# The first stages of a fused gated-scan and butterfly-FFN kernel: coefficient parts stacked over lanes, loads and fold steps reordered

## What is computed

```python
def step(r, kv_t):                       # over time
    r = 0.9 * r + kv_t
    return (r, r)
kv = ctx * ctx
x = x + layernorm(x) * scan(step, kv)    # gate
h = layernorm(x) @ W_exp + b_exp
h = butterfly(h, up_weights, 2048)       # 11 stages of pairs i, i ^ 2**stage
h = gelu(h + up_bias)
h = butterfly(h, down_weights, 2048)
x = x + h @ W_con + b_con + down_bias
```

## Time and profile before

| what | value |
|---|---|
| median of 3 runs | 2817.45 us (2816.68 to 2817.59) |
| the profiled execution | 2817.23 us, of which span 2815.4 us |
| mean granted TensorE clock | 0.986 |
| TensorE busy | 2752.3 us, 98% |
| VectorE, ScalarE, GpSimd busy | 2135.5, 1144.9, 396.0 us |
| moved | 540.4 MB, mean 192 GB/s |

### The profile page before, as it was taken

One profiled execution on the slowest core, in us unless ns is written; L12 is line 12 of the kernel. 1 busy time (PEld: TensorE's weight loads), 2 busy tenths in 40 slices (PEclk: granted clock), 3 DMA queues, 4 the chain that ended last, 5 costly groups with the idle time before them and its releaser, 6 DMA issues.

```text
span 2815.4 us, 35216 instructions
## 1 busy us (share of the span) xinstructions
PE 2752.3 (98%) x12281; PEld 2276.5 (81%) x12281; DVE 2135.5 (76%) x3568; ACT 1144.9 (41%) x1690; POOL 396.0 (14%) x568
## 2 busy tenths in 40 slices
PE   7859999999999999999999999999999999999999
PEld 6738888888888888888888888888888888888887
DVE  7867778787877878787787878777787877788533
ACT  6643443434344343434334343433434343343432
POOL 4531102010110101011010101111010111102000
PEclk7879999999999999999999999999999999999999
DMA  8696484856757585665748566574856657585542
GB/s 207 166 319 189 156 239 152 226 176 191 209 169 228 152 239 164 200 206 169 222 153 249 163 198 200 176 211 154 250 165 201 204 168 215 151 248 164 182 150 98
DMA packets 293924, 540.44 MB, mean 192 GB/s; under 512 B 38718, under 2 KB 102366, under 8 KB 276854
## 3 DMA queue, kind: packets, MB, share of 16 engines
q1 hardware_dynamic: 287382, 534.80, 62.6%
q0 software_dynamic: 1520, 2.27, 0.4%
q10 hardware_dynamic: 4848, 1.13, 0.2%
HBM read 447.89 MB, written 56.62 MB: 179 GB/s over the span
## 4 chain that ended last, share of the span: by engine, by line
PE 94%; DVE 2%; SPq 1%; DMA 1%; ACT 1%; issue 0%; POOL 0%; DVEq 0%; ACTq 0%
PE ps L1482 43%; PE ps L1500 25%; PE ps L1513 25%; PE ps L1343 1%; DMA HX<-in_L_ffn_up_weights_dram 1%; ACT W1f L741 0%; SPq L450 0%; DVE w1r L998 0%; PE ps L1393 0%; PE ps L1382 0%; DMA w1r<-w_products 0%; SPq L429 0%; DMA w_products<-xop 0%; DVE raw L1100 0%; SPq L456 0%
## 5 line engine op out<-in xcount | busy, mean ns | idle before, releaser
L1482 PE MATMUL ps<-xop,w1r 128*128 128x512 f32 x5376 | 1365.1, 389 | 10.0 <-DMA w1r<-w_products 6.1
L1482 PEld LDWEIGHTS ps<-xop,w1r 128*128 128x128 f32 x5376 | 1009.9, 188 | 221.5 <-DMA w1r<-w_products 6.5
L1500 PE MATMUL ps<-w2r,ghi 128*128 128x512 f32 x2048 | 630.5, 389 | 0.0
L1513 PE MATMUL ps<-w2r,ghi 128*128 128x512 f32 x2032 | 626.4, 389 | 0.0
L854 ACT ACTIVATE st<-ps 128x512 f32<-128x512 f32 x384 | 229.8, 598 | 844.3 <-PE ps L1482 843.4
L1184 DVE TENSOR_TENSOR x<-ps,x 128x512 f32<-128x512 f32 x508 | 349.0, 687 | 281.7 <-PE ps L1513 279.1
L1500 PEld LDWEIGHTS ps<-w2r,ghi 128*128 128x128 f32 x2048 | 384.5, 188 | 79.7
L1513 PEld LDWEIGHTS ps<-w2r,ghi 128*128 128x128 f32 x2032 | 382.1, 188 | 79.3
L1202 DVE TENSOR_TENSOR g<-ps,st 128x512 f32<-128x512 f32 x384 | 263.1, 685 | 215.9 <-PE ps L1482 215.4
L858 ACT ACTIVATE g<-g,gelu_bias 128x512 f32<-128x512 f32 x384 | 275.4, 717 | 364.2 <-DVE g L1202 364.2
L1207 DVE TENSOR_TENSOR glo<-g,ghi 128x512 fp32r<-128x512 f32 x510 | 345.6, 698 | 78.3 <-ACT ghi L872 78.2
(11 more groups left out here) (140 smaller groups left out, 1659.5 us busy)
## 6 DMA issues: line engine op xcount, KB each, us to landing
w1r<-w_products SPq DMA_DIRECT2D x889, 256.0 KB, 3.2
w2r<-w_split SPq DMA_DIRECT2D x128, 1024.0 KB, 5.0
x<-in_x_dram SPq DMA_DIRECT2D x128, 256.0 KB, 7.1
raw<-kv SPq DMA_DIRECT2D x496, 64.0 KB, 2.1
out_dram<-x SPq DMA_DIRECT2D x120, 256.0 KB, 4.0
kv<-in_ctx_dram SPq DMA_DIRECT2D x64, 256.0 KB, 7.4
raw<-in_ctx_dram SPq DMA_DIRECT2D x64, 256.0 KB, 5.0
w_split<-w2s SPq DMA_DIRECT2D x12, 512.0 KB, 3.3
```

What stands on the lines that cost most here:

```text
L1482: last = nc.tensor.matmul(bank[:, :], w1r[:, slot, w, c * P:(c + 1) * P], xop[:, XPOS[m], v, c, :], start=(opens and i == 0), stop=(i == l ...
L1500: last = nc.tensor.matmul(ps_ya[j][:, :], g[:, p % 2, q, j * P:(j + 1) * P], w2r[:, p % 2, kk, w, :], start=(p == 0 and kk == 0 and i == 0 ...
L1513: last = nc.tensor.matmul(ps_yb[:, :], g[:, p % 2, q, j * P:(j + 1) * P], w2r[:, p % 2, kk, w, :], start=(kk == 0 and i == 0), stop=(kk == ...
```

## The change

- The parted coefficients: the high part goes to lanes 0 to 31 and the remainder to lanes 32 to 63 of one buffer, with the lanes of 0 to 31 zeroed first (VectorE for up, GpSimd for down, semaphore `parts_zeroed`) and the rounded `sel` copied to both lane groups. One matmul over 36 or 34 lanes replaces two; the buffer holds the pair's two halves one behind the other, so VectorE reads the spread result, and ScalarE and VectorE the source, with a stride. `csrc_c` is gone.
- The up set's coefficients and top move from SP's queue to the head of ScalarE's; the four W_exp quarters stand first on SP. The up set's high coefficients move from SP's to GpSimd's queue, ahead of the down set's. hc_up and the bias broadcasts are issued later by ScalarE.
- TensorE does up's high spread before low_up instead of behind it. ScalarE does coefs_hi(1) and the first square inside low_up, VectorE coefs_lo(1) and high_products(0) around the first scans.
- All high_dn and back copies go to ScalarE. GpSimd does rstd_rows(1) ahead of the first weight sums, and the bias additions only when eight low_dn steps are done.
- SP stores product sets 2 and 3 before the second moves. The second load of w2 and the first loads of context in the main part are issued behind reloads of w1.
- VectorE's token sums and remainders are put later among low_dn's steps.

The core of the diff, with "..." for what is left out:

```diff
@@ SP
-            load_wexp(0)
-            load_coefs(sp, up_w, 0)
-            load_top(sp, up_w, 0)
-            for q in range(1, 4):
+            for q in range(4):
                 load_wexp(q)
             load_tokens(kv, 0, ctx_rows, 0, ctx_loaded[0])
             load_tokens(xs[0], 0, x_rows, 0, x_loaded[0])
             load_top(sp, down_w, 1)
-            load_high(sp, up_w, 0)
...
             store_w1(0)
             store_w1(1)
+            store_w1(2)
+            store_w1(3)
             sp.wait_ge(xn_turned, 2 * J)
             move_xT(sp, 1, 0, xT_moved[1])
             move_xT(sp, 1, 1, xT_moved[1])
-            store_w1(2)
-            store_w1(3)
...
             load_w2(0)
-            load_w2(1)
...
-                    if go and p == 0:
-                        if first:
-                            sp.wait_ge(first_moved[1], FIRST_MOVES * NX)
+                    if go and p == 0 and not first:
                         sp.wait_ge(xT_moved[1], moved_by(u))
                         load_tokens(kv, 0, ctx_rows, u * 2 + 2, ctx_loaded[0])
                     for m in range(NM):
                         refill(u, p, m, last)
-                        if go and p == 0 and m == NM - 1:
+                        if first and p == 0 and m == 3:
+                            sp.wait_ge(first_moved[1], FIRST_MOVES * NX)
+                            sp.wait_ge(xT_moved[1], moved_by(u))
+                            load_tokens(kv, 0, ctx_rows, u * 2 + 2, ctx_loaded[0])
+                        if go and p == int(first) and m == (2 if first else NM - 1):
                             sp.wait_ge(xlo_ready, (u + 1) * NM)
                             load_tokens(raw[:, 1, :, :], 0, ctx_rows, u * 2 + 3, ctx_loaded[1])
...
-                    if not (first and p == 0) and not (last and p >= NP - 1):
+                    if first and p == 0:
+                        load_w2(1)
+                    elif not (last and p >= NP - 1):
@@ GpSimd
+            load_high(pool, up_w, 0)
             load_coefs(pool, down_w, 1)
+            pool.wait_ge(coef_spread, LOWS)
+            nc.gpsimd.memset(parts_zero(1), 0.0).then_inc(parts_zeroed, 1)
             load_high(pool, down_w, 1)
...
             first_moves(0)
+            rstd_rows(1)
             wait_kept(pool, "high_up", R - 1)
             weight_sums(0)
-            rstd_rows(1)
             weight_sums(1)
...
             pool.wait_ge(bias_row_ready, 1)
+            wait_kept(pool, "low_dn", KH // 2)
             add_bias(0, 0, xs[0])
@@ ScalarE
+            load_coefs(act, up_w, 0)
+            load_top(act, up_w, 0)
             act.dma_start(bias_rows[0:KH, :], ...)
             act.dma_start(bias_rows[KH:2 * KH, :], ...)
-            act.dma_start(hc_up, ...)
-            act.dma_start(bias_row[:, :], ...)
-            act.dma_start(bias_tmp, ...)
...
                 if k == KH // 4:
                     coefs_hi(0)
+                    act.dma_start(bias_row[:, :], ...)
+                    act.dma_start(bias_tmp, ...)
                     pick(0)
-                    coefs_hi(1)
                 fold_step("WT", k)
-            square(0, 0)
             for k in range(KH):
+                if k == 2:
+                    square(0, 0)
+                if k in (5, 8):
+                    coefs_hi(1, k // 8)
                 fold_step("low_up", k)
             pick(1)
             square(0, 1)
+            act.dma_start(hc_up, ...)
@@ VectorE
-            coefs_lo(1)
...
-            for j in range(J):
-                scan_chunk(0, 0, j)
+            scan_chunk(0, 0, 0)
+            scan_chunk(0, 0, 1)
+            coefs_lo(1)
+            scan_chunk(0, 0, 2)
+            scan_chunk(0, 0, 3)
+            high_products(0)
             stats1(0, 0, xs[0], range(J))
...
-            high_products(0)
             for j in range(J):
                 normalise(0, 0, xs[0], j)
...
-            fold_step("high_dn", 3)
...
-            fold_step("high_dn", 7)
...
-            for k in range(KH // 2):
-                fold_step("back", k)
             weights_lo(4)
-            for k in range(KH // 2, KH):
-                fold_step("back", k)
             tokens_lo(0, 0)
             tokens_lo(0, 1)
             weights_lo(5)
             token_sum(0, 0, first=True)
-            token_sum(0, 1, first=True)
             for k in range(4):
                 fold_step("low_dn", k)
             weights_lo(6)
+            token_sum(0, 1)
             for k in range(4, 8):
                 fold_step("low_dn", k)
             tokens_lo(0, 3)
-            token_sum(0, 2, first=True)
-            token_sum(0, 3, first=True)
             weights_lo(7)
             for k in range(8, KH):
                 fold_step("low_dn", k)
-            for m in (5, 2, 4, 6):
-                tokens_lo(0, m)
+            token_sum(0, 2)
+            tokens_lo(0, 5)
+            tokens_lo(0, 2)
+            token_sum(0, 3)
+            tokens_lo(0, 4)
+            tokens_lo(0, 6)
@@ TensorE
+                def parted_spread(place, stage):
+                    rows, off, n = src_place(stage)
+                    bank = place[0]
+                    for c in range(n // 1024):
+                        for bit in range(2):
+                            at = off + bit * (n // 2) + c * 512
+                            last = nc.tensor.matmul(ps[bank + c][:, :], sel_r[dn][0:Q + rows, stage - PARTED[0], bit, :],
+                                                    low_parts[dn][0:Q + rows, at:at + 512],
+                                                    start=(bit == 0), stop=(bit == 1))
+                    last.then_inc(coef_spread, 1)
...
+            spread_high()
             pe.wait_ge(low_matrix_ready, 1)
             for k in range(KH):
                 wait_kept(pe, "WT", k)
                 fold_step("low_up", k)
-            spread_high()
             spread_low_dn()
```

More of the change, by code:

```diff
@@ L299, in xattn_ffn_program, with low_part, low_whole, parts_zero @@
         PARTED = range(LOWS - 2, LOWS)
+        def low_part(dn, stage, lane):
+            rows, off, n = src_place(stage)
+            return low_parts[dn][lane:lane + rows, off:off + n].rearrange("q (b x) -> q b x", b=2)
+        def low_whole(dn, stage):
+            rows, off, n = src_place(stage)
+            return low_src[dn][0:rows, off:off + n].rearrange("q (x b) -> q b x", b=2)
+        def parts_zero(dn):
+            first, last = src_place(PARTED[0])[1], sum(src_place(PARTED[-1])[1:])
+            return low_parts[dn][0:Q, first:last].bitcast(f32)
         def spreads(dn, stage):
@@ L750, in coefs_hi @@
                     act.wait_ge(coef_spread, LOWS)
[L751 to L754 removed]
+                act.wait_ge(parts_zeroed, dn + 1)
+                for stage in PARTED if only is None else [PARTED[only]]:
+                    act.activation(low_part(dn, stage, 0), low_whole(dn, stage), ACT.Copy).then_inc(coef_hi, 1)
             def weights_hi(n):
@@ L947, in path_products @@
                         for c in range(banks):
-                            coef = ps[bank + c][:, col:col + m].rearrange("p (o a l) -> p o a l", o=outer // banks, a=2)
+                            order = "p (o l a) -> p o a l" if not first and stage in PARTED else "p (o a l) -> p o a l"
+                            coef = ps[bank + c][:, col:col + m].rearrange(order, o=outer // banks, a=2)
                             last = path_stage(nc.vector, cur[:, c * m:(c + 1) * m],
```

67 lines of the change are left out of this document (27 added, 40 removed).

## The result

The changed kernel takes **2823.62 us** (median of 12 runs, 2821.29 to 2827.72), the kernel before 2817.30 (12 runs, 2815.17 to 2818.63) on the same chip: a ratio of 1.0024, 95% interval 1.0015 to 1.0033. It is slower, by 0.24%. The forecast was 2805.4 with a range up to 2812.5: wrong in sign, and outside its range. The profiled execution took 2825.76 us, 2.1 over its median, with a span of 2824.0 us (before 2815.4).

A forecast was written before the change was run, and what follows sets the result against it. All behind 213.60 us, where TensorE's waits stop, was taken as constant. +6.4, -5.7 and -7.3 bring products 6.6 us earlier; with the end, that point becomes 201.8: 2817.2 - 11.8 = 2805.4 us, range 2797 to 2812.5.

The forecast's parts named there:

- wexp: Start: last wexp quarter, landing at 32.15 before, taken to land at 25 with hc_up and two bias broadcasts moved later.
- the path that the forecast said gives less: Before high_dn: later VectorE scans and statistics, then GpSimd's order holding ScalarE's first split to 111.1, against 113.0 by wcon.
- (a): Rival, start: wexp lands at 32, low_up starts 3 to 4 us later and all after it; 2809.4, chance 0.20.
- (b): Rival: front not late, as top lands as before or the clock holds, and token work overlaps; 2799.4, chance 0.17.
- (c): Rival, end: stores set it, last store stays near 194 and only 5.2 us count; 2812, chance 0.08.
- (d), the clock: Rival: TensorE at half clock in low_up, high_up and high_dn; 40 of 48 steps so would give 2836.4, chance 0.05.
- The middle: From first high_dn copy, ScalarE does all copies without wait: 38.7 us against 44.4, -5.7; then -7.3 to low_dn's last remainder.
- hc_up beside wcon: hc_up's packets issued beside the wcon load: between nothing and 5.4 us, taken as 2; wcon lands at 110.9.
- Stacking: In each spread 12 matmuls of 512 columns become 6, 2.7 us of TensorE covered by other waits: nothing gained.
- The end: Behind the first products: token instructions take 10.6 us against 4.63; first reloaded product at 197.7, no stall, 2.6 us half clock gone.
- My -7.3 for the late order: From split 5 to low_dn's last remainder, 34.2 us before: two token sums leave (4.3), the split falls from 5.3 to 2.3.

The follow-up runs named there:

- base: Changed kernel with up's six coefficient loads and top back on SP between the first and second wexp quarter: 2811.58 us, ratio 0.9979 to the kernel before.
- the runs on GpSimd's loads: Changed kernel with GpSimd waiting for up's coefficients to land before it issues its loads of up's high coefficients: 2823.03 us, ratio 1.0022 to the kernel before.

## Why the prediction was wrong, point by point

| point | forecast | changed kernel | base (coefs on SP) |
|---|---|---|---|
| low_up starts | 35.0 | 46.33 | 33.33 |
| wait for wcon ends | 110.9 | 120.49 | 107.65 |
| first products | 178.6 | 189.89 | 176.09 |
| third product after the first | 6.7 | 9.75 | 9.74 |
| first reloaded product | 197.7 | 211.98 | 198.82 |
| span | 2803.6 | 2824.0 | 2807.1 |

**The step that failed** is in the loads: "The top coefficients (2 MB) now share with wexp instead of preceding its last three quarters: pick(0) waited for them to 18.59, I take 20.7." It came at 29.02, 8.3 us later. And the sentence passes over the coefficients themselves, six loads of 16 KB that the first spread waits for: I gave them no later arrival at all, though the same edit takes them out of the same order. They came at 20.61, and by VectorE's rows that alone would have held its pick until 28.24. Either lateness without the other would have cost within 0.8 us of the same; the runs moved both together. I had computed what the sharing does to wexp, the transfer that gains, and too little or nothing for those that give way. With both back in the order, or with the bulk held until they had landed, the spread starts at 10.69 and 10.12, low_up at 33.33 and 32.56, and the time is 2811.58 and 2812.56 us.

low_up missed by 11.3 us: 8.3 by top, and 3.0 between the pick and low_up, in a part of the sum that is not the loads'. VectorE's copy of top took 3.83 us (before 1.98), so the top matrix was ready 7.4 us after the pick began, not 6.3; and the last nine steps of WT took 9.0 us, where I had 0.5 for each. Why is open: 1.00 of the clock was granted there. In the two other profiled executions with this start (the runs on GpSimd's loads and on the context) low_up was 12.4 and 12.9 us behind the forecast, with top at 33.10 and 33.2. The miss of 11.3 is part of the 20.4 us by which the span (2824.0 for 2803.6) missed, and on the way down it is +9.6 at the wait for wcon, +11.4 at the first high_dn copy (124.38 for 113.0) and +11.3 at the first products. At high_dn it comes by the path that the forecast said gives less: ScalarE had waited 2.46 us there for GpSimd's sums.

**wexp** was read rightly in kind: a quarter late at 32.15 is not late any more. In the base its wait ends at 27.58, against my 25.

**Rivals.** (a) had the sharing as its ground, with the wrong victim: it left wexp at 32 and forecast 3 to 4 us. The Trainium skill's rule, on the page DMA: Bandwidth & Descriptors, section Issuing engines are not separate DMA queues, that loads interleave on the same engines whoever issues them, agrees with the run that held the bulk back. I used it for wexp alone. (b) did not occur. (c) did in part: the first reload was to be issued 9.7 us after the first product and was at 203.84, 13.95 after it, since SP waited 2.7 us for w2's stores and 4.5 for w1's. Its share in the miss is hidden, for the product was late as well and found its weights there. (d), the clock, did not in the size that it needed: five steps of low_up took 6.19 us, with 0.50 granted from 46 to 49, where they take 4.73 in the run with the context load early, but over whole folds the granted clock was 0.92 in low_up (before 1.00), 0.87 in high_up (0.84) and 0.87 in high_dn (0.87). The slower outcome, to which I gave 0.05, came by a mechanism that I had not among the rivals.

**The middle** held. From the first high_dn copy (124.38) to the end of split 5 (163.74) it is 39.4 us, forecast 38.7, before 44.4. From there to the first products 26.2, forecast 26.9. For hc_up beside wcon I took 2 us: the wcon load took 44.7 us here and 44.9 in the base, 43.9 before and 45.2 at most in any run, so 1.3 or less. In the base the wcon wait ends 3.2 us ahead of the forecast mainly because pick(1), which the load waits for, ended at 62.80 and not at 65.0. Stacking cost nothing that a row shows: 16 + 6 matmuls in 7.7 us (20.61 to 28.33), and a memset of 2.62 us in VectorE's idle time. It was not undone by itself, and neither was the move of the copies to ScalarE.

**The end** was mis-sized. The third product was to come 6.7 us after the first and came at 9.75; the first reloaded product at 19.1 after and came at 22.1: +3.0. The third product's operand was ready 4.9 us after the first product, so the token chain is not what held it. ScalarE's product copy is: in its program it stands behind its last two token parts, and then it waited 1.80 us for a w2 store (198.90). Of the 3.05 us that is 1.8, and 1.25 are the order. My -7.3 for the late order is right up to the first product (8.6 measured by undoing it) but is worth 4.7 in the time.

**The context** has no term in the forecast. Moving its load behind reloads made VectorE's scan, which stands ahead of the addition to x, late: 3.66 us of wait and 1.7 of lower clock. Who waits for a load that is moved back belonged in the sum.

11.3 + 3.0 + 5.4 = 19.7 of the 20.4 us, and the steady part adds 0.6. The time itself missed by 18.2 us, since the profiled execution is 2.1 over its median. Executions of the base range from 2809.02 to 2814.48, and its profiled one is the lowest. By medians the base still misses the forecast by 6.2 us: 1.1 at the first reloaded product, 2.1 from there on (1.84 of it the wait), 2.6 between its profiled run and its median; the last 0.4 stays open. So even without the harm of the queue the forecast was too good by that much.

## What to carry to other kernels

In this kernel the order within one queue worked as a priority, and a second queue gave it up: top was there at 13.75 us behind one quarter of wexp in one queue, and at 29.02 from the head of a queue of its own beside the bulk. Before a load moves to a queue of its own, ask what order it had, and what bulk will now run beside it; if it must move, hold the bulk until it has landed (2812.56 us here, against 2823.62). And where several chains end near each other, as here behind 175 us, time taken out ahead of them may pay only until the next one (stores, context, reload). Price the second and third wait before adding up what the first is worth.

## What the runs showed of the hardware that was not expected

- Issuing can block the issuer: 42.54 us for one issue on ScalarE's queue behind 2 MB and some 4100 small packets, 6.10 behind the packets alone, 0.35 with neither ahead. That what is queued ahead is the cause is read from the order of the issues.
- Six loads of 16 KB, issued by 6.1 us, took until 20.6 to land beside bulk in another queue. With that bulk held back they had landed by 9.62, 4 us behind the last issue.
- During the wcon load, from 70 to 90 us, the core moves 108 to 115 GB/s with 0.50 to 0.57 of the DMA engines' time taken, and 121 to 125 with all of it, the load in more and smaller transfers. The stores behind 150 reach 393 to 409 GB/s.
- The last wexp quarter lands between 26.47 and 29.95 in seven profiled executions with the same start. This spread, 3.5 us, is the size of what the last experiments tried to tell apart.
